# Neighbour-maximum stage: the row gathers of a tile are paced by all eight transpose steps

## The chip, the cores and the metric

The kernel runs on one core of one Trainium2 chip. The metric is device time in microseconds (us), median of several executions. Engines are named as in the profile: PE (TensorE), DVE (VectorE), ACT (ScalarE), POOL (GpSimd), SP (SyncE, here only DMA issues).

## What is computed

Four graph layers run over 8192 nodes with 128 features and one 8192 x 8192 adjacency matrix `adj` of int32 (about 33 neighbours in a row: each off-diagonal entry is set with probability 0.0039). Layer 0 is the one that the change touches; layers 1 to 3 are attention layers over the same mask.

```python
# layer 0: maximum over the neighbours, feature by feature
vals = jnp.max(jnp.where(mrows[:, :, None], X[None, :, :], neg), axis=1)
out  = jnp.where(has_nbr[:, None], vals, 0)
x = _layernorm(x + out)
# layer 1: attention with a threshold; layers 2 and 3: plain masked attention
attention = softmax(where(adj > 0, leaky_relu(s_i + s_j), NEG)) ; h = attention @ (x @ W)
x = _layernorm(x + elu(h))
```

## The kernel before

**The stage.** `neighbour_max` works in 64 row tiles of 128 nodes. PE transposes a tile of `adj` (1 MB a piece, four pieces) in eight steps `e` = 0 to 7 of eight 128x128 blocks (`turn`, L474), ACT turns each step's block into an fp8 mask (`stage`, L430), and every fourth tile the mask of four tiles goes to DRAM for the later layers. Neighbours are handled in groups of 16 columns ("words"). The first neighbour of each word is selected with matrix products: PE marks it (`first_ps`, L493), ACT makes it a 0/1 matrix (`lone`, L417), PE multiplies x with it (`sums`, L507), and DVE folds the result into a running maximum `top` (`pair`, L607, eight per tile, one per step). These are for the quad of four tiles before. Words with more than one neighbour leave neighbours over; DVE extracts up to 24 of them per node as row numbers (`idx`, L686 to L774), and POOL fetches these rows of x by indirect DMA into `ring` (24 slots of 128x128 fp32, one gather a slot, L356). DVE reduces `ring` by a tree of maxima (`larger`, L612, seven per tile) and writes the result (`into`, L619, two per tile).

**The order around the gathers.** PE, ACT and DVE go through phases, one per tile, each written out by hand as eight steps. DVE's phase t does three things interleaved: eight `pair` operations, the extraction of tile t-1, and the tree of tile t-3. POOL runs a loop over tiles, `tile(t, k)`. For tile t it waits until the indices exist (`idx_ready`) and then fills three ranges of the ring, each after the tree of tile t-1 has let it go:

- slots 6 to 11 ("upper"), free after the first L612 of a DVE phase (`upper_free`);
- slots 0 to 5 ("lower"), free after the first L619 (`lower_free`), after step 1;
- slots 12 to 14 ("rest"), free after the second L619 (`rest_free`), between steps 4 and 5;
- slots 15 to 23, three conditional groups of 2, 2 and 5 slots: gathered if any node of the tile needs them, else filled with -3e38 by a memset (L392).

`follow(part)` holds POOL until PE has finished `t * 8 + 16 + part` transpose steps: `part` = 0 is satisfied when PE's phase t+1 is over, `part` = p when step p-1 of phase t+2 is. The last two tiles are not paced.

**What waits for the gathers.** DVE's tree of tile t runs in phase t+3. Its first L612 waits for the twelve upper and lower gathers (`gathered`). Its fourth L612 (written at L726, after step 3) waits for `rest_ready`, which POOL gives in `report()`: that call waits until the rest and conditional gathers of the tile before have landed, and stands inside the next tile's program, between its upper and its lower gathers. Nothing but DVE waits for a gather; POOL's waits are for DVE and PE.

Of the kernel before, what the change touches and what calls it, by code (L numbers as in the profile page):

```python
# [33 lines left out]
HALF = SLOTS // 2  # L34
# [44 lines left out]
def hold(eng, sem, value):  # L79


    eng.wait_ge(sem, value)
    if not isinstance(value, int):
        eng.sem_inc(SPARE[0], 1)
# [96 lines left out]
def neighbour_max(nc, x, adj, mask_t, x_ext, nm, deg, consts, constants):  # L181
# [14 lines left out]
    with ExitStack() as ctx:  # L196
# [76 lines left out]
        gathered = sem("gathered")  # L273
# [21 lines left out]
        @block.sync  # L295
        def _(sp):
            for h in range(PIECES):
                sp.dma_start(adjb[:, h, :], adj[0:P, h * PW:(h + 1) * PW]).then_inc(adj_in[h], 16)

            def rows(t):  # L300

                for h in range(PIECES):

                    hold(sp, transposed, (t - 1) * 8 + (h + 1) * HT)
                    sp.dma_start(adjb[:, h, :], adj[bass.ds(t * P, P), h * PW:(h + 1) * PW]).then_inc(adj_in[h], 16)

            for t in range(1, TC):
                for k in SPLIT_BEHIND[t]:
                    quarter = slice(k * T // XQ, (k + 1) * T // XQ)
                    sp.dma_start(nm[:, quarter, :], x.rearrange("(t p) f -> p t f", p=P)[:, quarter, :]).then_inc(x_in[k], 16)  # L310
                rows(t)
            with sp.Fori(TC, T) as t:
                rows(t)

            sp.wait_ge(transposed, T * 8)
            sp.dma_start(x_again, x.rearrange("(t p) f -> p t f", p=P)).then_inc(x_back, 16)
            sp.wait_ge(flag_ready, 1)
            more = sp.value_load(flag[0:1, 0:1], min_val=0, max_val=1)
            with sp.If(more != 0):
                with sp.Fori(0, T) as t:  # L320
                    hold(sp, fb_adj_used, t + 1)
                    sp.dma_start(fb_rows, adj[bass.ds(t * P, P), :]).then_inc(fb_adj, 16)
                    with sp.Fori(0, N // FJ) as s:
                        hold(sp, fb_step, (t * (N // FJ) + s) * 3 + 1)
                        sp.dma_start(
                            xb, x[bass.ds(s * FJ, FJ), :].rearrange("j f -> (j f)").partition_broadcast(P),
                        ).then_inc(fb_x, 16)

        @block.gpsimd
        def _(pool):  # L330

            constants_on_pool(pool)
            pool.wait_ge(adj_in[PIECES - 1], 16)
            blocks = lambda ap: ap.rearrange("(a two p) f -> a two p f", two=2, p=P)
            for odd in range(2):
                pool.dma_start(blocks(x_ext[0:N, :])[:, 1 - odd], blocks(x)[:, odd]).then_inc(x_copied, 16)
            pool.wait_ge(low_ready, 1)
            pool.dma_start(x_ext[N:N + P, :], top[:, 0, 0:F]).then_inc(low_in, 16)
            sel_steps = Steps(pool, sel_made)
            sel_steps.do(nc.gpsimd.memset(sel[:, :, :], 0.0))  # L340
            for k in range(3):
                rows = range(3 * k, (3, 6, 7)[k])
                for at in range(0, P, 32):
                    for r in rows:
                        sel_steps.do(nc.gpsimd.affine_select(out=sel[:, k, :], in_=sel[:, k, :], compare_op=ALU.not_equal, fill=1.0, base=-(at + r), pattern=[[0, 1]], channel_multiplier=1))
            pool.wait_ge(x_copied, 32)
            pool.wait_ge(low_in, 16)
            blanks = Tally(pool, blanked, 1)
            extra = Tally(pool, low_in, 16)
            pool.sem_inc(blanked, 1)  # L350
            for free in (upper_free, lower_free, rest_free):
                pool.sem_inc(free, 1)

            def gather(k, first, number, done):
                for s in range(first, first + number):
                    pool.indirect_dma_start(ring[:, s, :], None, x_ext,  # L356
                                            bass.IndirectOffsetOnAxis(ap=idx[:, k, s:s + 1], axis=0)).then_inc(done, 16)

            def report():

                extra.wait(0)
                blanks.wait(0)
                pool.sem_inc(rest_ready, 1)

            def tile(t, k, paced=True):

                def follow(part):
                    if paced:
                        hold(pool, transposed, t * 8 + LATER * 8 + part)

                hold(pool, idx_ready, t + 1)
                hold(pool, upper_free, t + 1)
                for part in range(2):
                    follow(part)
                    gather(k, HALF // 2 + 3 * part, 3, gathered)
                report()
                hold(pool, lower_free, t + 1)
                for part in range(3):
                    follow(2 + part)
                    gather(k, 2 * part, 2, gathered)  # L380
                hold(pool, rest_free, t + 1)
                gather(k, FIRST[1], SIZES[1], low_in)
                pool.reg_add(extra.reg, extra.reg, 16 * SIZES[1])
                hold(pool, need_in, t + 1)
                for g in range(SURE, GROUPS):
                    rows = pool.value_load(need_i[0:1, k, g - SURE:g - SURE + 1], min_val=0, max_val=P)
                    with pool.If(rows != 0):
                        gather(k, FIRST[g], SIZES[g], low_in)
                        pool.reg_add(extra.reg, extra.reg, 16 * SIZES[g])
                    with pool.If(rows == 0):  # L390

                        nc.gpsimd.memset(ring[:, FIRST[g]:FIRST[g] + SIZES[g], :], -BIG).then_inc(blanked, 1)  # L392
                        pool.reg_add(blanks.reg, blanks.reg, 1)

            with pool.Fori(0, T // 2 - 1) as it:
                tile(it * 2, 0)
                tile(it * 2 + 1, 1)
            tile(T - 2, 0, False)
            tile(T - 1, 1, False)
            report()  # L400
            pool.wait_ge(x_back, 16)
            for quad in range(NC - 1):
                at = slice(quad * TC, (quad + 1) * TC)
                pool.wait_ge(rows_step, quad + 1)
                nc.gpsimd.tensor_tensor(out=nm[:, at, :], in0=nm[:, at, :], in1=x_again[:, at, :], op=ALU.add).then_inc(x_added, 1)
            pool.wait_ge(missed_ready, 1)
            nc.gpsimd.partition_all_reduce(missed_all[:, :], missed[:, :], P, bass.bass_isa.ReduceOp.max).then_inc(missed_shared, 1)
# [1584 lines left out]
```

## Time and profile before

| | |
|---|---|
| median of 3 executions | 4901.41 us (4897.9 to 4901.55) |
| span of the profiled execution | 5439.8 us |
| layer 0 in it | about 0 to 2240 us |
| layers 1 to 3 in it | about 2240 to 5440 us |
| busy in the span | PE 84%, DVE 79%, ACT 41%, POOL 22% |
| POOL | 1051 gathers, 148 memsets in the ring |

The profiled execution is 538.4 us longer than the median of the timed ones, so intervals in it can't be carried over to the timed ones without a look at where that time lies. Idle time of an engine that is not the bottleneck costs nothing; "issue" means that the engine waited for nothing the profile shows, and "remote" means that what released it wasn't found among the records near by.

### The profile page before, as it was taken

The numbers are of one execution on the slowest core, as the hardware profiler recorded it, in microseconds if no ns is written. First come the engines' busy times: TensorE is split into PE (matmuls) and PEld (weight loads), VectorE is DVE, ScalarE is ACT, GpSimd is POOL, SyncE is SP. The second block draws the span as 40 slices with busy tenths as digits, with TensorE's granted clock in tenths as the row PEclk, the third lists the DMA queues.
The fourth block names the chain that finished last, engine by engine and source line by source line (L and its number), as shares of the span: only waits on it lengthen the run. The fifth ranks groups of instructions, "written<-read, shape, count | busy, mean of one in ns | idle before, by whom it ended". The sixth has DMA issues, their size and how long they took to land. (4 is left out here: it accounts for less than half of the span.)

```text
span 5439.8 us, 68010 instructions
## 1 busy us (share of the span) xinstructions
PE 4559.6 (84%) x22263; PEld 2172.7 (40%) x22263; DVE 4311.2 (79%) x7371; ACT 2207.6 (41%) x2430; POOL 1205.9 (22%) x1342
## 2 busy tenths in 40 slices
PE   4766776677667766579999999999999999999999
PEld 3333333333333333323443333454444445444444
DVE  6666676667666667788888888889999987999998
ACT  3444444444444444398888888410000001000000
POOL 5555445454444455200000000000000000000000
PEclk6888888888888889889999999999999999999999
DMA  7555555555555555233232332122222202212220
GB/s 272 195 187 184 192 197 185 187 182 194 186 179 188 193 169 166 95 130 122 105 126 111 113 127 105 64 102 83 75 84 79 81 9 99 102 70 98 76 96 14
DMA packets 181695, 709.72 MB, mean 130 GB/s; under 512 B 31168, under 2 KB 39872, under 8 KB 132224
## 3 DMA queue, kind: packets, MB, share of 16 engines
q1 hardware_dynamic: 110816, 566.01, 29.3%
q0 software_dynamic: 33760, 73.21, 4.2%
q10 hardware_dynamic: 36864, 67.13, 3.5%
q8 instruction: 157, 2.57, 0.2%
q14 instruction: 98, 0.80, 0.0%
HBM read 630.59 MB, written 79.82 MB: 131 GB/s over the span
## 5 line engine op out<-in xcount | busy, mean ns | idle before, releaser
L1750 PE MATMUL bank<-w,GX 128*128 128x512 f32 x4096 | 1768.4, 593 | 4.8 <-DVE w L1865 4.8
L1865 DVE SCALAR_TENSOR_TENSOR w<-q,E,m 128x512 f32<-128x512 f32 x2048 | 1472.1, 758 | 130.8 <-PE bank L1750 39.1
L356 POOL DMA_INDIRECT ring<-x_ext,idx x1051 | 1032.8, 983 | 1074.2 <-DVE X L619 316.8
L1750 PEld LDWEIGHTS bank<-w,GX 128*128 128x128 f32 x4096 | 777.7, 191 | 975.3 <-issue 975.2
L607 DVE TENSOR_TENSOR top<-top,sums 128x1024 f32<-128x1024 f32 x484 | 589.2, 1217 | 626.7 <-remote 364.8
L507 PE MATMUL sums<-lone,xs 128*128 128x512 fp8e4 x3000 | 838.3, 421 | 287.0 <-DVE top L607 214.9
L1200 PE MATMUL acc<-w,GX 128*128 128x512 f32 x2048 | 939.6, 605 | 65.8 <-DVE w L1458 62.6
L430 ACT ACTIVATE stage<-tp 128x1024 fp8e4<-128x1024 uint16 x512 | 523.7, 1025 | 1088.1 <-remote 598.3
L1458 DVE SCALAR_TENSOR_TENSOR w<-q,E,u 128x1024 f32<-128x1024 f32 x512 | 634.7, 1274 | 1.9 <-PE acc L1200 1.8
L507 PEld LDWEIGHTS sums<-lone,xs 128*128 128x128 bf16 x3000 | 291.5, 105 | 814.7 <-issue 607.4
L1200 PEld LDWEIGHTS acc<-w,GX 128*128 128x128 f32 x2048 | 371.9, 190 | 564.5 <-issue 413.5
L417 ACT ACTIVATE lone<-first_ps 128x1024 fp8e4<-128x1024 f32 x512 | 522.3, 1020 | 83.1 <-PE first_ps L493 39.3
L1231 ACT ACTIVATE above<-q,nd 128x1024 fp8e4<-128x1024 f32 x488 | 516.7, 1142 | 0.0
L1242 ACT ACTIVATE u<-ell,ndd 128x1024 fp8e4<-128x1024 f32 x448 | 478.1, 1141 | 43.7 <-DVE w L1458 43.4
L493 PE MATMUL first_ps<-stage,firsts 128*128 128x512 fp8e4 x1022 | 343.7, 421 | 144.4 <-ACT lone L417 125.2
L474 PE MATMUL tp<-ident_b,adjb 128*128 128x128 bf16 x4096 | 361.8, 237 | 121.0 <-issue 54.6
L1762 ACT ACTIVATE num<-bank 128x512 f32<-128x512 f32 x32 | 19.1, 597 | 1006.4 <-PE bank L1750 1006.4
L1715 POOL TENSOR_TENSOR lone_part<-mean_w,nohas 128x512 f32<-128x512 f32 x32 | 37.7, 1180 | 1583.8 <-DVEq L1823 1561.1
L474 PEld LDWEIGHTS tp<-ident_b,adjb 128*128 128x128 bf16 x4096 | 276.5, 106 | 163.2 <-issue 71.2
L486 PE MATMUL tally<-powers,stage 128*128 128x16 bf16 x4096 | 169.9, 171 | 143.1 <-ACT stage L430 99.4
L486 PEld LDWEIGHTS tally<-powers,stage 128*128 128x128 fp8e4 x4096 | 163.9, 99 | 255.4 <-ACT stage L430 124.5
L612 DVE TENSOR_TENSOR ring<-ring 128x128 f32<-128x128 f32 (+2 forms) x448 | 251.2, 561 | 6.2 <-DMA ring<-x_ext,idx 3.6
(250 smaller groups left out, 2919.3 us busy)
## 6 DMA issues: line engine op xcount, KB each, us to landing
adjb<-in_adj SPq DMA_DIRECT2D x256, 1024.0 KB
m<-mask_t SPq DMA_DIRECT2D x128, 1024.0 KB, 4.8
mask_t<-stage ACTq DMA_DIRECT2D x256, 256.0 KB
den_m<-mask_t SPq DMA_DIRECT2D x64, 1024.0 KB, 6.9
keep_m<-mask_t SPq DMA_DIRECT2D x64, 1024.0 KB, 4.9
ring<-x_ext,idx POOLq DMA_INDIRECT x1051
z<-row_scores SPq DMA_DIRECT2D x30, 256.0 KB, 4.6
xt_rows<-XT SPq DMA_DIRECT2D x8, 512.0 KB, 4.7
```

What stands on the lines that cost most here:

```text
L356: pool.indirect_dma_start(ring[:, s, :], None, x_ext, bass.IndirectOffsetOnAxis(ap=idx[:, k, s:s + 1], axis=0)).then_inc(done, 16)
L417: nc.scalar.activation(lone[:, b, :, :], first_ps[:, :, :], ACT.Relu, saturate=False).then_inc(lone_made, 1)
L430: nc.scalar.activation(stage[:, q, e * TRB:(e + 1) * TRB, k * P:(k + 1) * P], tp[e % 2][:, :, :].bitcast(U16), ACT.Sign, saturate=False).t ...
L474: last = nc.tensor.transpose(tp[e % 2][:, i, :], low_half[:, j // PW, j % PW:j % PW + P], ident_b[:, :])
L507: last = nc.tensor.matmul(out[:, a, :], xs[:, part_, 2 * n + a, :], lone[:, b, a, :], start=(part_ == 0), stop=(part_ == 2))
L607: nc.vector.tensor_tensor(out=top[:, :, :], in0=top[:, :, :], in1=sums, op=ALU.max).then_inc(sums_used, 1)
L1200: last = nc.tensor.matmul(acc[:, h, :], GX[:, j, :], w[:, n % WR1, h, :], start=(j == 0), stop=(j == T - 1))
L1231: nc.scalar.activation(above[:, n % AS, :, i, :], qb[:, c % 2, :, :], ACT.Sign, bias=nd[:, j:j + 1], scale=-1.0, saturate=False).then_inc( ...
L1242: nc.scalar.activation(u[:, n % US, :, i, :], ell[:, c % 2, :, :], ACT.Sign, bias=ndd[:, j:j + 1], saturate=False).then_inc(keeps_made, 1)
L1458: nc.vector.scalar_tensor_tensor(out=w[:, n % WR1, :, :], in0=qb[:, c % 2, :, :], scalar=E[:, j:j + 1], in1=u[:, n // GT % US, :, j % GT, ...
L1750: last = nc.tensor.matmul(acc[b][:, :], GX[:, j, :], w[:, j % WR, :], start=(j == 0), stop=(j == T - 1))
L1865: nc.vector.scalar_tensor_tensor(out=w[:, j % WR, :], in0=q, scalar=E[:, j:j + 1], in1=m[:, b, j, :], op0=ALU.max, op1=ALU.mult).then_inc( ...
```

## The change

Only `tile` in POOL's program changes. The upper slots go in three pairs behind steps 0, 1 and 2 of PE's phase (before: two lots of three, behind the end of the phase before and behind step 0), and `report()` is called after the second pair, that is after four upper gathers and not after six. The lower slots go in pairs behind steps 3, 4 and 5 (before: 1, 2 and 3). The rest group gets a wait for step 6 on top of `rest_free`, and the conditional groups a wait for step 7, the last of the phase.

```diff
                 hold(pool, upper_free, t + 1)
-                for part in range(2):
-                    follow(part)
-                    gather(k, HALF // 2 + 3 * part, 3, gathered)
-                report()
+                for part in range(3):
+                    follow(1 + part)
+                    gather(k, HALF // 2 + 2 * part, 2, gathered)
+                    if part == 1:
+                        report()
                 hold(pool, lower_free, t + 1)
                 for part in range(3):
-                    follow(2 + part)
+                    follow(4 + part)
                     gather(k, 2 * part, 2, gathered)
                 hold(pool, rest_free, t + 1)
+                follow(7)
                 gather(k, FIRST[1], SIZES[1], low_in)
                 pool.reg_add(extra.reg, extra.reg, 16 * SIZES[1])
                 hold(pool, need_in, t + 1)
+                follow(8)
                 for g in range(SURE, GROUPS):
```

In the built program this is POOL's order from the top of a tile in the loop, before. `transposed` is PE's count of steps, `low_in` and `blanked` are what `report()` waits for.

```order
L82 ISA [waits idx_ready,upper_free]
L356 DMA ring<-x_ext,idx 128x128 [waits transposed]
L356 DMA ring<-x_ext,idx 128x128 x2
L82 REGISTER_ALU
L356 DMA ring<-x_ext,idx 128x128 [waits transposed]
L356 DMA ring<-x_ext,idx 128x128 x2
L82 REGISTER_ALU [waits low_in,blanked,lower_free]
L356 DMA ring<-x_ext,idx 128x128 [waits transposed]
L356 DMA ring<-x_ext,idx 128x128
L82 REGISTER_ALU
```

And the same place now:

```order
L82 ISA [waits idx_ready,upper_free]
L356 DMA ring<-x_ext,idx 128x128 [waits transposed]
L356 DMA ring<-x_ext,idx 128x128
L82 REGISTER_ALU
L356 DMA ring<-x_ext,idx 128x128 [waits transposed]
L356 DMA ring<-x_ext,idx 128x128
L82 REGISTER_ALU [waits low_in,blanked]
L356 DMA ring<-x_ext,idx 128x128 [waits transposed]
L356 DMA ring<-x_ext,idx 128x128
L82 REGISTER_ALU [waits lower_free]
```

The report has moved ahead of the last two upper gathers, and these have a wait of their own. Further down in POOL's tile, at the rest group and the first conditional one, this stood before:

```order
L356 DMA ring<-x_ext,idx 128x128 [waits rest_free]
L356 DMA ring<-x_ext,idx 128x128 x2
L383 REGISTER_ALU
L386 TENSOR_LOAD need_i [waits need_in]
L386 ISA x2
```

And now:

```order
L82 REGISTER_ALU [waits rest_free]
L356 DMA ring<-x_ext,idx 128x128 [waits transposed]
L356 DMA ring<-x_ext,idx 128x128 x2
L385 REGISTER_ALU
L82 REGISTER_ALU [waits need_in]
L389 TENSOR_LOAD need_i [waits transposed]
L389 ISA x2
```

Both groups now wait for a step of PE after the wait that they had. No instruction of PE, DVE, ACT or SP moves.

## Rows read from the trace of the kernel before

**Rows 1.** The page: length of the profiled execution.

```profile
span 5439.8 us, 68010 instructions
```

**Rows 2.** Busy time of each engine in a stretch of layer 0, granted clock, DMA share.

```profile
500.00:1000.00 500.00, 350.14 (x2852) 180.41 (x2851) 340.37 (x711) 234.51 (x265) 249.70 (x279) 0.87 0.55 188
```

**Rows 3.** Groups by line, 0 to 2400 us: count, busy, mean; idle before, releasers.

```profile
L356 POOL DMA_INDIRECT ring<-x_ext,idx x1051 | 1032.8, 983 | 1074.2 <-DVE X L619 316.8 <-issue 306.5 <-DVE ring L612 193.2
...
L607 DVE TENSOR_TENSOR top<-top,sums 128x1024 f32<-128x1024 f32 x484 | 589.2, 1217 | 626.7 <-remote 364.8 <-PE sums L507 227.2 <-issue 33.0
```

**Rows 4.** Waits of DVE, 200 to 2100 us: total, times, longest.

```profile
DVE top L607 <- remote: 335.8, 90, 10.1
DVE top L607 <- PE sums L507: 206.2, 205, 3.1
```

**Rows 5.** Line 356, the gathers: durations min/median/max, and who waited for them.

```profile
L356 POOL DMA_INDIRECT ring<-x_ext,idx x1051: 938/944/3283, 41.0 to 2193.7; - x176
...
who waited for it (us, times):
  DVE ring L612: 3.6, 1
```

**Rows 6.** Tile X and line 711: durations min/median/max, first and last start.

```profile
L619 DVE TENSOR_TENSOR X<-ring x64: 278/280/851, 78.8 to 2205.7; 128x128 f32<-128x128 f32 x64
...
L711 DVE TENSOR_SCALAR keys<-codes x64: 413/426/552, 22.2 to 2148.3; 128x512 int32<-128x512 int32 x64
```

**Rows 7.** Timeline around 1010 us: start, us, engine, line.

```profile
1001.20 0.95 DVE L612 TENSOR_TENSOR ring<-ring 128x768 f32<-128x768 f32 x1
...
1005.71 0.61 PE L474 MATMUL tp<-ident_b,adjb 128*128 128x128 bf16 x8
...
1006.23 0.94 POOL L356 DMA_INDIRECT ring<-x_ext,idx  x1 [7.13 <-DVE X L619]
...
1009.13 0.61 PE L474 MATMUL tp<-ident_b,adjb 128*128 128x128 bf16 x8
...
1013.69 0.95 DVE L612 TENSOR_TENSOR ring<-ring 128x768 f32<-128x768 f32 x1
...
1014.64 0.61 PE L474 MATMUL tp<-ident_b,adjb 128*128 128x128 bf16 x8
...
1021.33 0.61 PE L474 MATMUL tp<-ident_b,adjb 128*128 128x128 bf16 x8
1021.37 1.21 DVE L607 TENSOR_TENSOR top<-top,sums 128x1024 f32<-128x1024 f32 x1
```

**Rows 8.** The same timeline a few steps on.

```profile
1029.96 1.02 ACT L430 ACTIVATE stage<-tp 128x1024 fp8e4<-128x1024 uint16 x1 [9.28 <-remote]
...
1030.08 1.22 DVE L607 TENSOR_TENSOR top<-top,sums 128x1024 f32<-128x1024 f32 x1 [5.70 <-remote]
...
1030.72 0.94 POOL L356 DMA_INDIRECT ring<-x_ext,idx  x1 [2.37 <-remote]
```

**Rows 9.** Timeline of DVE, first phase after the last transposes.

```profile
2141.81 0.95 DVE L612 TENSOR_TENSOR ring<-ring 128x768 f32<-128x768 f32 x1
...
2149.39 1.21 DVE L607 TENSOR_TENSOR top<-top,sums 128x1024 f32<-128x1024 f32 x1
...
2153.56 0.95 DVE L612 TENSOR_TENSOR ring<-ring 128x768 f32<-128x768 f32 x1
```

**Rows 10.** Timeline of POOL, the same phase, and after the last gather.

```profile
2143.52 0.95 POOL L356 DMA_INDIRECT ring<-x_ext,idx  x1 [5.17 <-DVE ring L612]
...
2147.27 0.96 POOL L356 DMA_INDIRECT ring<-x_ext,idx  x1 [0.30 <-issue]
...
2149.87 0.94 POOL L356 DMA_INDIRECT ring<-x_ext,idx  x1 [0.30 <-issue]
...
2158.13 0.94 POOL L356 DMA_INDIRECT ring<-x_ext,idx  x1 [0.30 <-issue]
...
2196.67 16.90 POOL L405 TENSOR_TENSOR X<-X,adjb 128x512 f32<-128x512 f32 x12 [0.86 <-DMA ring<-x_ext,idx]
```

## The prediction

> **What bounds the kernel now.** I read the span first, then the busy times of a stretch of layer 0, then the groups by line, then who waits for whom, and last the timeline of single phases. Only layer 0 holds gathers; the three layers behind it are not touched by an instruction and are taken as they are.
>
> The profiled execution takes 5439.8 us [rows 1], 538.4 us more than the median of 4901.41 us. In layer 0 the first L619 of a tile starts 64 times between 78.8 and 2205.7 us [rows 6], so a phase takes (2205.7 - 78.8) / 63 = 33.8 us in the trace. A phase without disturbance can be pieced together from the rows. From the start S of a phase (the first L612, three quarters of 1024 wide) to the fourth L612 (L726, after step 3) DVE needs 2153.56 - 2141.81 = 11.75 us [rows 9]; that phase has no transposes, but its first part takes as long as one that has them: 7.58 us to the `pair` of step 2 there, 1021.37 - 1013.69 = 7.68 us here [rows 7, 9]. From L726 to the next phase's start DVE needs 1013.69 - 1001.20 = 12.49 us [rows 7]. Together 24.2 us. The missing 9.6 us of a phase are in holes: at 1021.94 us PE ends a transpose step, and ACT, DVE and POOL start again only at 1029.96, 1030.08 and 1030.72, all three put down to "remote" [rows 7, 8]. DVE's waits of that kind sum to 335.8 us [rows 4]. Such holes over 63 phases are 63 x 9.6 = 605 us, near the 538.4 us by which the profiled execution is longer. So I take nearly all of the holes to be absent from the timed executions. A timed phase is then about 33.8 - 538.4 / 63 = 25.2 us.
>
> What fills it is DVE: it is busy 340.37 of 500 us in the trace [rows 2], 68% of 33.8 us, that is 23.0 us of work per phase, 91% of 25.2 us. The rest is mostly DVE waiting for PE's sums (206.2 us over some 56 phases, holes included, all of it before L607) [rows 3, 4]. POOL is busy 250 of 500 us, 16.9 us a phase [rows 2], its idle time before gathers is put down to DVE's L619 and L612 first [rows 3], and DVE waited for a gather once, 3.6 us [rows 5]. So layer 0 goes at DVE's pace with PE close behind, and POOL has about 8 us a phase to spare. A change of POOL's order counts only if it makes DVE wait, or ends a wait of DVE.
>
> **The change part by part.** All times are from S; a timed phase ends at S + 25.2 and its undisturbed bound is S + 24.2.
>
> *Upper gathers.* POOL's first one starts at 2143.52, S + 1.71 (0.76 us after that L612 ended), and then one every 1.25 us [rows 9, 10]. PE's step 1 ends at 1014.64 + 0.61 = S + 1.56, step 3 at 1021.33 + 0.61 = S + 8.25 [rows 7]; step 0 is over before S, and step 2 lies between, near S + 5. The new gates ask for step 0 before the pair at S + 1.7, step 1 before that at S + 4.2 and step 2 before that at S + 6.7. All are open when POOL comes to them. Cost 0.
>
> *The report.* It came after the sixth gather, whose start is 2149.87 and end 2150.81, S + 9.0; DVE asks at S + 11.75, so the margin is 2.75 us and DVE did not wait. Now it comes after the fourth, 2147.27 + 0.96, S + 6.4, margin 5.3 us [rows 9, 10]. Gain 0 where there was no wait. The one tile whose big conditional group was gathered (148 memsets of 192 leave 44 gathered groups, and 1051 - 960 = 91 gathers in them make 43 groups of two and one of five) may have had one: at most the 3.6 us of [rows 5], once.
>
> *Lower gathers.* Before, the sixth started at 2158.13, S + 16.3, and ended at S + 17.3 [rows 10]. The gates now are step 3 (S + 8.25), step 4 (a step is 24.2 / 8 = 3.0 us, S + 11.3) and step 5 (S + 14.3), against pairs that started at S + 9.3 (2149.87 + 1.25), S + 11.8 (two gathers on) and S + 15.1 (2158.13 - 1.25). An open gate costs nothing; a gate that POOL waits at lets it go about 1 us later (0.76 us from the end of the L612 to the first upper gather above). So the last pair may slip from S + 15.1 to S + 15.3, and end at S + 17.6. What is the landing? After POOL's last gather (start 2193.7 [rows 5], end 2194.6) it waited until 2196.67 for the data, memsets in between, so landing is at most 2.1 us [rows 10]. The twelve are there at S + 19.7, and DVE asks for them at S + 24.2 at the earliest: margin 4.5 us. Cost 0. The Trainium skill says in "Perfetto Trace Analysis" (the part on the DMA instruction of the software path) that the profiler's end of such an instruction is the end of descriptor generation and not the arrival of the data; the row on 2196.67 agrees, which is why the 2.1 us stand in the margin.
>
> *Rest group.* `rest_free` let POOL start at 1006.23, 5.03 us after L726, hence S + 16.8, or at S + 17.6 when the lower gathers end later. Step 6 ends at 1005.71 + 0.61, 5.12 us after L726, S + 16.9 [rows 7]. If POOL has to wait there, it starts 1 us later, S + 17.9: a slip of 0.3 to 1.1 us, with 3 x 1.25 us of gathers behind it, end S + 21.6. Nobody waits for them before S + 24.2 + 11.75. Cost 0.
>
> *Conditional groups.* Step 7 ends at 1009.13 + 0.61 = 8.54 us after L726, S + 20.3 [rows 7], before POOL gets there. With memsets (about 1.2 us) POOL is done at S + 22.8, with one gathered pair (2.5 us more) at S + 25, with two at S + 27. The next upper gathers can't start before S + 24.2 + 1.7 = S + 25.9. Queued behind this wait on POOL are those next upper gathers and the report; the worst common case pushes them by 1 us against a margin of 5.3 us. Cost 0 in 63 tiles, and 0 to 5 us once in the tile with nine extra gathers.
>
> *Added waits themselves.* Three more register waits a tile on POOL, some tenths of a us each, in 8 us of spare time: 0.
>
> The bounds: a row that shows a paced gather making DVE wait does not exist, so its cost is bounded above by the 1 us that a closed gate takes, if all of it reached DVE in every phase, 62 us; the bound below is the part of a timed phase over the undisturbed one, 25.2 - 24.2 = 1.0 us a phase, 63 us, if smoother gathers removed all of it. I take 0, since every margin is over 4 us. Sum: 5439.8 + 0 for a profiled execution, 4901 us timed (before's own spread is 3.7 us; what can be told from no change is about 0.2%, 10 us).
>
> One rule speaks for more than that. A gather takes 0.94 us as a rule and up to 3.28 us [rows 5], so something blocks POOL at times; the one DVE operation of 0.43 us per phase of the tensor-scalar kind, L711, takes 0.41 to 0.55 us [rows 6]. The Trainium skill, "SBUF — State Buffer", Who interferes with whom, says that a VectorE operation in a two-port mode and GpSimd exclude each other from a shared port pair, the loser standing still. By that rule a moved gather can lose or gain one L711, 0.4 us of POOL's spare time, and DVE at most 0.14 us a phase (0.55 - 0.41), 9 us in all; the upper gathers lie under L711 before and after, so neither changes here.
>
> **The rivals.** *R1, faster: bursts of gathers are what holds the others up.* The holes lie at steps 3 and 4, after POOL has issued eight or more gathers in a row, and the steps in which POOL is idle are quick. If part of this is real in timed executions, pairs spread over the phase would give it back. The pot is the 1.0 us a phase: all of it 63 us, 4838 us; a third to a half, 4870 to 4880 us. Against it: the gates are open when POOL comes, so the burst of twelve is hardly broken up; it decides only if PE's steps come later than POOL's pace, above all where a hole has already begun. *R2, slower: the gates bind and DVE waits.* Place: the last lower pair behind step 5 and the first L612 of the next phase. If PE in timed executions runs late against DVE (its clock is granted at 0.87 on the mean here [rows 2]) by more than 4.5 us at step 5, each phase pays the excess; 0.5 us a phase gives 31 us, 4932 us. Against it: DVE waits for each step's sums, so PE can't be a whole step and a half behind. *R3, slower: the conditional groups next to the phase change.* 44 groups; if each moved the report past its margin by 0.5 us it would be 22 us, 4923 us. It decides once POOL is more than 5.3 us late, which only the nine-gather tile is. *R4: the change does in effect nothing*, gates open throughout: that is the forecast, with no difference in time.
>
> **How the numbers follow.** Forecast and R4 together 0.53, at 4901 us, own range 4893 to 4910. R1 0.29, R2 0.12, R3 0.06. The range takes most of R1 and the near half of R2 and R3: 4868 to 4922. Faster by over 0.2%: 0.29; within 0.2%: 0.53; slower: 0.18.
>
> **What would show it.** In the changed profile: the sixth upper gather of a tile still 6.4 us after the first; the first L612 and L726 of a phase with no wait for a gather or POOL; POOL's waits before L356 moving from L619 and L612 towards PE's L474; 1051 gathers and 148 memsets; undisturbed pieces of 11.75 and 12.5 us as before. The place and size of the holes may differ, and with them the profiled span, without a change in the timed median. The forecast is wrong if the undisturbed pieces change, if DVE waits for a gather in many phases, or if the timed median moves with the holes; the last would say that the holes are in the timed executions too.

## The result, and the profile after

The changed kernel takes 4924.65 us (median of 4; 4922.01 to 4927.49) against 4901.48 us before: ratio 1.0044, 95% interval 1.0029 to 1.0059. Measured once more beside the last experiments it is 4924.21 us, ratio 1.0049 (1.0036 to 1.0063). It is slower by 20 to 24 us, outside the range forecast. Ratios and intervals here and below are of undisturbed executions: one of the kernel before (5138 us) and two of the variant b_stt (7550 and 13435 us) were slow and are left out of them, and the median of b_stt without those two is 4896.66 us.

Its profiled execution takes 4921.2 us and has no holes, so the trace that stands ahead of the prediction can't be compared with it row by row. The kernel before was profiled again, unchanged ("b_again" below), this time without holes: 4900.3 us. "Before" in the rows from here on is this second trace. The two pages, first the changed kernel, then before:

```profile
span 4921.2 us, 68382 instructions
```

```profile
span 4900.3 us, 68010 instructions
```

DVE's waits from 200 to 1600 us, changed kernel and then before (us in total, times, longest). In place of the 335.8 us "remote" and 206.2 us for PE's sums of [rows 4] there is this:

```profile
DVE top L610 <- PE sums L510: 90.6, 165, 3.6
DVE ring L615 <- DMA ring<-x_ext,idx: 1.5, 2, 1.2
```

```profile
DVE top L607 <- PE sums L507: 84.9, 168, 3.2
DVE ring L612 <- DMA ring<-x_ext,idx: 3.1, 1, 3.1
```

DVE waits 5.7 us more for PE's sums, which comes back at the end of this document, and less than before for gathers: no wait explains 23 us. What grew most is the duration of one tiny DVE operation, which writes the 128x3 flags `need` and stands between the last `pair` of a phase and `idx`. These are its rows by line (min/median/max in ns; L771 in the changed kernel, L768 before):

```profile
L771 DVE TENSOR_SCALAR need<-srt x64: 158/182/1628, 31.1 to 1660.0; 128x3 bf16<-128x3 f32 x64
```

```profile
L768 DVE TENSOR_SCALAR need<-srt x64: 156/164/1630, 31.0 to 1637.2; 128x3 bf16<-128x3 f32 x64
```

The medians hide it. Over 0.3 us it takes in 30 of 64 tiles after and in 20 before, and summed over its own median it has 23.3 us too much after, 9.4 us before. The timeline of one tile with one gathered pair shows where it comes from. Changed kernel, end of a tile (start, us, engine, line):

```profile
686.68 0.61 PE L477 MATMUL tp<-ident_b,adjb 128*128 128x128 bf16 x8
687.14 0.94 POOL L356 DMA_INDIRECT ring<-x_ext,idx  x1 [0.30 <-issue]
...
688.71 0.94 POOL L356 DMA_INDIRECT ring<-x_ext,idx  x1 [0.62 <-issue]
...
689.96 0.94 POOL L356 DMA_INDIRECT ring<-x_ext,idx  x1 [0.31 <-issue]
690.68 0.18 DVE L769 SCALAR_TENSOR_TENSOR base<-srt,four 128x24 int32<-128x24 int32 x1
690.86 0.97 DVE L771 TENSOR_SCALAR need<-srt 128x3 bf16<-128x3 f32 x1
690.90 0.90 POOL L395 MEMSET ring<- 128x256 f32 x2
...
691.99 0.95 DVE L615 TENSOR_TENSOR ring<-ring 128x768 f32<-128x768 f32 x1
```

The same place before, in another tile with one gathered pair:

```profile
172.44 0.61 PE L474 MATMUL tp<-ident_b,adjb 128*128 128x128 bf16 x8
172.83 0.94 POOL L356 DMA_INDIRECT ring<-x_ext,idx  x1 [0.30 <-issue]
174.07 0.94 POOL L356 DMA_INDIRECT ring<-x_ext,idx  x1 [0.30 <-issue]
175.32 0.94 POOL L356 DMA_INDIRECT ring<-x_ext,idx  x1 [0.30 <-issue]
176.26 0.90 POOL L392 MEMSET ring<- 128x256 f32 x2
...
176.63 0.56 DVE L768 TENSOR_SCALAR need<-srt 128x3 bf16<-128x3 f32 x1
...
177.35 0.95 DVE L612 TENSOR_TENSOR ring<-ring 128x768 f32<-128x768 f32 x1
```

The line of a memset x2 stands for two of them, 128x256 (group of two) and 128x640 (group of five). In both kernels the small operation ends within 0.05 us of the end of the second one (691.80 and 177.16): DVE stands until POOL has finished. Before, the memset is 0.37 us ahead of the operation and costs it 0.4 us; after, it starts 0.04 us behind, directly after a gather, and costs 0.8 us. Everything behind it on DVE, the next phase included, starts later by as much. In the tiles without a gathered pair the memsets are over before L771 in both kernels (0.17 us).

That it is the memset and not the gather ahead of it can be seen in three tiles of the changed kernel in which more than one conditional group is gathered. There a gather ends 0.04 us behind the start of the operation, just as above, but another gather follows it and no memset, and the operation takes 0.17 us; with memsets behind the gather it takes 0.95 to 0.97 us, in 25 tiles. One of the three:

```profile
333.14 0.94 POOL L356 DMA_INDIRECT ring<-x_ext,idx  x1 [0.30 <-issue]
334.04 0.17 DVE L771 TENSOR_SCALAR need<-srt 128x3 bf16<-128x3 f32 x1
334.39 0.94 POOL L356 DMA_INDIRECT ring<-x_ext,idx  x1 [0.30 <-issue]
```

Why the memset is later is seen at POOL's sequencer. It loads the flag of each conditional group, branches, and goes on to the next. These are its three loads in the two tiles above, changed kernel and then before (the times are the first and last start):

```profile
L389 POOLq TENSOR_LOAD <-need_i x3: 283/291/293, 687.4 to 690.1; - x3
```

```profile
L386 POOLq TENSOR_LOAD <-need_i x3: 284/287/296, 170.4 to 173.0; - x3
```

Before, the sequencer runs ahead of the engine: the loads start at 170.4, under the first rest gather and 3.7 us before the first conditional one (174.07), and the last of them is done before that one starts. After, the sequencer stands at the new wait for step 7, whose last transposes end at 687.29, and only then begins: first load at 687.4, last at 690.1. The first conditional gather starts 0.62 us after the rest group (0.30 before).

This moves the end of the memsets by 0.4 us in the tiles in which they lay on the operation before too. In seven tiles (counted from 0: 15, 19, 31, 35, 43, 51 and 60) they were over 0.24 us ahead of the operation before, and now they lie on it for 0.97 us. In six of the seven the operation stands at the end of the first phase of a quad, and in such a phase the new gates do hold POOL. These are the third upper pair and the first lower pair in the phase that ends with the operation of tile 15, changed kernel:

```profile
418.30 0.94 POOL L356 DMA_INDIRECT ring<-x_ext,idx  x1 [1.24 <-PE tp L477]
...
421.56 1.26 POOL L356 DMA_INDIRECT ring<-x_ext,idx  x1 [1.07 <-PE tp L477]
```

A second difference is at the start of the kernel. DVE's waits from 60 to 110 us, the changed kernel and then before:

```profile
DVE ring L615 <- DMA ring<-x_ext,idx: 7.3, 2, 5.5
```

```profile
DVE ring L612 <- DMA ring<-x_ext,idx: 3.6, 1, 3.6
```

The first gather starts at 50.7 us and not at 41.0 us, since the first tile's upper pair now needs step 0 of phase 2, and PE's early phases wait for the adjacency tiles to come in. DVE's first `pair` starts at 103.9 us against 101.1 us.

### The profile page after: what moved, and what is told of

It reads as the page before. It is cut to its first block and busy times, and to the rows that moved or that the text cites. A ratio compares the mean times of both kernels' runs of the same rounds, so it can differ in the third digit from the quotient of the medians.

```text
span 4921.2 us, 68382 instructions
## 1 busy us (share of the span) xinstructions
PE 4381.2 (89%) x22263; PEld 2106.9 (43%) x22263; DVE 4321.6 (88%) x7371; ACT 2210.7 (45%) x2430; POOL 1232.6 (25%) x1342
## 5 line engine op out<-in xcount | busy, mean ns | idle before, releaser
L356 POOL DMA_INDIRECT ring<-x_ext,idx x1051 | 1060.2, 1009 | 507.7 <-issue 295.4
L510 PE MATMUL sums<-lone,xs 128*128 128x512 fp8e4 x3000 | 742.1, 384 | 261.7 <-DVE top L610 237.7
L510 PEld LDWEIGHTS sums<-lone,xs 128*128 128x128 bf16 x3000 | 262.6, 98 | 740.0 <-issue 441.3
L477 PE MATMUL tp<-ident_b,adjb 128*128 128x128 bf16 x4096 | 327.0, 225 | 71.0 <-DVE X L633 38.0
L496 PE MATMUL first_ps<-stage,firsts 128*128 128x512 fp8e4 x1022 | 311.0, 386 | 0.3 <-ACT lone L420 0.3
L477 PEld LDWEIGHTS tp<-ident_b,adjb 128*128 128x128 bf16 x4096 | 254.1, 101 | 102.5 <-DVE X L633 41.3
L615 DVE TENSOR_TENSOR ring<-ring 128x128 f32<-128x128 f32 (+2 forms) x448 | 250.5, 559 | 15.4 <-DMA ring<-x_ext,idx 12.8
L1769 ACT ACTIVATE ex<-ex 128x512 f32<-128x512 f32 x32 | 20.2, 630 | 540.0 <-DVE ex L1827 540.0
```

The lines of the kernel that those rows point to most:

```text
L356: pool.indirect_dma_start(ring[:, s, :], None, x_ext, bass.IndirectOffsetOnAxis(ap=idx[:, k, s:s + 1], axis=0)).then_inc(done, 16)
L477: last = nc.tensor.transpose(tp[e % 2][:, i, :], low_half[:, j // PW, j % PW:j % PW + P], ident_b[:, :])
L510: last = nc.tensor.matmul(out[:, a, :], xs[:, part_, 2 * n + a, :], lone[:, b, a, :], start=(part_ == 0), stop=(part_ == 2))
```

## The experiments

Changes are against the kernel named. Excess means the time by which the small operation (L768 or its line in the variant) takes longer than its own median in that trace, summed over the tiles in which it does.

**b_again, the kernel before, unchanged, one execution.**

> The kernel before, unchanged, profiled once more to get a phase without the holes that its first trace had. Theory A (collision: POOL's memset of a conditional group holds up DVE's small tensor-scalar L768, as it does in 30 tiles of the changed kernel, 0.98 us in place of 0.17): span near 4900 us, L768 long in fewer than 10 tiles or by clearly less, phases shorter than after's by 0.37 us on the mean. Theory B (the later gathers land later and DVE waits for data): L768 as long as after's, and L612 waits for the gathers' DMA less than the 12.8 us in the changed kernel.

Measured: 4902.06 us, span 4900.3 us. From DVE's first `pair` to the next phase's, a phase takes 25.2 us on the mean (25.5 us in the changed kernel). The operation is long in 20 tiles, not fewer than 10, but at 0.56 us in most and not 0.97 us. The wait of DVE for gathers is less than after (10.7 against 12.8 us in all), a difference of 2 us that lies at the start. Theory A is favoured, with a part of the cost already in the kernel before.

**no8, the changed kernel without the wait for step 7.**

```diff
                 hold(pool, need_in, t + 1)
-                follow(8)
                 for g in range(SURE, GROUPS):
```

> The changed kernel without the wait for step 7 ahead of the conditional groups. The wait adds 0.30 us between the rest gathers and the conditional ones (0.61 us against 0.31 us) although its step is long over. Theory A: the memsets come 0.3 us earlier against L771, which then takes 0.67 us in place of 0.97 us in about 28 tiles: 8 us less, 4916 us. Theory B (late data): under 2 us less.

Measured: 4915.17 us, ratio to before 1.0026 (1.0017 to 1.0035). The operation takes 0.64 to 0.67 us in 24 tiles; excess 14.2 us, 9 us less than after; the time is 9 us less. As A said.

**no78, without the waits for steps 6 and 7.**

```diff
                 hold(pool, rest_free, t + 1)
-                follow(7)
                 gather(k, FIRST[1], SIZES[1], low_in)
                 pool.reg_add(extra.reg, extra.reg, 16 * SIZES[1])
                 hold(pool, need_in, t + 1)
-                follow(8)
                 for g in range(SURE, GROUPS):
```

> The changed kernel without the waits for steps 6 and 7: what is left of the change is the pairs behind later steps and the early report. Theory A: the memsets come 0.4 us earlier, L771 loses some 0.35 us in 28 tiles, not 0.8 us: 4912 to 4914 us, unless the chain ahead of it moves too. Theory B: 4922 us or so if the later lower pairs are what costs, 4901 us if the rest group is.

Measured: 4908.03 us, ratio 1.0013 (1.0004 to 1.0022), better than the 4912 to 4914 us expected: the operation is at 0.56 us again, but in 28 tiles and not 20 (excess 12.4 us, 3 us over before). The seven tiles named above are among them, so the later gates of the pairs are enough to bring the memsets onto the operation there (0.56 to 0.57 us). The upper and lower gates and the early report together are worth 7 us at most: nearly 3 us are the start and 3 us this. Against no8 the time is 7 us less, while the excess is only 2 us less; the profiled executions of the two take equally long in layer 0 (1594 and 1595 us from the first `pair` to the last), so what else the wait for step 6 costs, if anything, isn't shown.

**a_stt, the changed kernel with the small operation in another form.** It compares twice, (srt < 1) < srt, which gives the same 0 or 1.

```diff
-nc.vector.tensor_scalar(need[...], srt[...], 1.0, None, ALU.is_ge)
+nc.vector.scalar_tensor_tensor(out=need[...], in0=srt[...], scalar=1.0, in1=srt[...],
+                               op0=ALU.is_lt, op1=ALU.is_lt)
```

> The changed kernel with the small DVE operation at L771 in another form that gives the same numbers (a scalar-tensor-tensor, which compares twice), everything else as it is. Theory A: if only the tensor-scalar form has to share with POOL's memset, the new one takes 0.17 us in all tiles, and the 23 us go: 4901 us or a little less. Theory B: no difference, 4924 us.

Measured: 4897.18 us, ratio 0.9991 (0.9982 to 1.0): all of the loss is gone. The same place in a tile, its timeline:

```profile
178.57 0.95 POOL L356 DMA_INDIRECT ring<-x_ext,idx  x1 [0.30 <-issue]
...
179.48 0.15 DVE L771 SCALAR_TENSOR_TENSOR need<-srt 128x3 bf16<-128x3 f32 x1
179.52 0.90 POOL L395 MEMSET ring<- 128x256 f32 x2
179.55 0.17 DVE L773 SCALAR_TENSOR_TENSOR base<-srt,base 128x24 int32<-128x24 int32 x1
```

```profile
L771 DVE SCALAR_TENSOR_TENSOR need<-srt x64: 151/157/193, 30.6 to 1631.0; 128x3 bf16<-128x3 f32 x64
```

The memset starts 0.04 us behind the operation, exactly as in the changed kernel, and the operation takes 0.15 us: at most 0.193 us in 64 tiles. All of POOL's work is where the change put it. This is the run that settles the cause.

**b_stt, the same edit in the kernel before.**

> The kernel before with the small DVE operation at L768 in its scalar-tensor-tensor form. In before's trace without holes L768 is long too: 0.56 us in 20 tiles, 9.4 us over its usual 0.16 us. Theory A (collision with the memset): these 9 us go, 4892 us. Theory B (the changed kernel lost 23 us through late data, and the other form only happened to win it back): no change, 4901 us.

Measured: 4897.75 us, ratio 0.9987 (0.9974 to 1.0). The direction is A's; the size, some 5 to 6 us, is less than the 9 us expected. With this form in both, the changed kernel (4897.18) and the one before (4897.75) can't be told apart.

**b_rev, the kernel before with the conditional groups in reversed order.**

```diff
-                for g in range(SURE, GROUPS):
+                for g in reversed(range(SURE, GROUPS)):
```

> The kernel before with the three conditional groups in reversed order: the group of five first, then the two of two. In tiles with one gathered pair (always the first of the two) the memsets then come before the pair and are over some 2 us ahead of L768, which keeps its form. Theory A: L768 takes 0.16 us in nearly all tiles, 4892 us. Theory C (it is the gathers and not the memsets that hold the operation up): the pair now lies over L768, which gets longer, 4901 us or more.

Measured: 4896.8 us, ratio 0.9985 (0.9976 to 0.9995). The expectation was right in time and half right in the trace: L768 is still long in 22 tiles, in 21 of them at about 0.4 us (excess 5.6 us), although no memset is near:

```profile
174.31 0.90 POOL L392 MEMSET ring<- 128x640 f32 x2
...
176.63 0.94 POOL L356 DMA_INDIRECT ring<-x_ext,idx  x1 [0.30 <-issue]
...
177.16 0.41 DVE L768 TENSOR_SCALAR need<-srt 128x3 bf16<-128x3 f32 x1
```

It ends with the gather (177.57): a gather holds it up too, theory C, but less than the memsets do, and only with its last part. In this trace the operation ends with the gather in 22 of the 23 tiles in which it starts 0.53 to 0.72 us into one, and takes its usual 0.16 to 0.17 us where it starts 0.05 to 0.33 us into one. The gain comes from moving the memsets off it.

**b_gate1, the kernel before with later gates for the upper gathers alone.**

```diff
                 for part in range(2):
-                    follow(part)
+                    follow(1 + part)
```

> The kernel before, its two upper lots of three behind steps 0 and 1 of PE's phase and not behind the end of the phase before and step 0. In the changed kernel the first tile's gathers start at 50.7 us and not at 41.0 us, and DVE waits 5.5 us for them and not 3.6 us. Start-up theory: the first pair of DVE comes some 2.5 us later here as there, L768 is as in before: 4904 us. If it is 4901 us, the start-up costs nothing; if it is 4910 us or more, the gates of the upper gathers cost in the other tiles too.

Measured: 4905.64 us, ratio 1.0009 (0.9996 to 1.0023): the time fits but alone can't be told from no change. The trace is clearer: first gather at 50.8 us, first `pair` at 104.2 us (101.1 before), excess of L768 8.2 us, no more than before. DVE's wait from 60 to 110 us:

```profile
DVE ring L612 <- DMA ring<-x_ext,idx: 7.0, 2, 4.3
```

**b_plus8, the kernel before with the wait for step 7 alone.**

```diff
                 hold(pool, need_in, t + 1)
+                follow(8)
                 for g in range(SURE, GROUPS):
```

> The kernel before with the wait for step 7 alone, ahead of the conditional groups. It should shift the memsets by 0.3 us towards the end of the tile. Theory A: L768 goes from 0.56 us to 0.87 us in the 20 tiles in which it was long, 6 us more: 4907 us. Theory B (late lower gathers): no change, 4901 us.

Measured: 4919.07 us, ratio 1.0027 (1.0018 to 1.0037). The wait does more than expected: the operation goes to 0.97 us in 25 tiles, excess 22.5 us, 13.1 us over before. One line makes most of the loss. It too brings the memsets onto the operation in the seven tiles in which they were ahead of it, at 0.96 us: either this wait or the later gates of the pairs is enough for that. Later gates for the upper gathers alone (b_gate1) leave it at 0.16 us in all seven.

```profile
174.85 0.95 POOL L356 DMA_INDIRECT ring<-x_ext,idx  x1 [0.69 <-issue]
176.10 0.94 POOL L356 DMA_INDIRECT ring<-x_ext,idx  x1 [0.30 <-issue]
...
177.00 0.97 DVE L769 TENSOR_SCALAR need<-srt 128x3 bf16<-128x3 f32 x1
177.04 0.90 POOL L393 MEMSET ring<- 128x256 f32 x2
```

The gap ahead of the conditional gather is 0.69 us and not the 0.61 us I had expected from a fixed cost: POOL is released by an event, the end of step 7, and lands in the same place whether the rest gathers end 0.1 us earlier or not. So the step was not "long over", as the expectation for no8 has it.

**a_loads, the changed kernel with the three flag loads ahead of the wait.**

```diff
+                wanted = [pool.value_load(need_i[0:1, k, g - SURE:g - SURE + 1], min_val=0, max_val=P) for g in range(SURE, GROUPS)]
                 follow(8)
                 for g in range(SURE, GROUPS):
-                    rows = pool.value_load(need_i[0:1, k, g - SURE:g - SURE + 1], min_val=0, max_val=P)
+                    rows = wanted[g - SURE]
```

> The changed kernel with the three loads of the conditional groups' flags ahead of the wait for step 7; the wait itself stays. Run-ahead theory: POOL's sequencer reaches this wait under the running rest gathers, at S + 18.5, and stands there until step 7 (S + 20.4); only then come three times load, check and branch, 0.9 us each, so that the last memset can't start before S + 24.0. With the loads done ahead it can: first conditional gather at S + 21.45, memset over 0.3 us earlier, L771 0.65 us, 4915 us as without the wait. Rival (the gate itself and its register arithmetic make the delay): no change, 4924 us.

Measured: 4914.05 us, ratio 1.0025 (1.0015 to 1.0035), what no8 has without the wait. The wait is there, behind the same step, and costs nothing of its own once the loads are ahead of it:

```profile
178.90 0.94 POOL L356 DMA_INDIRECT ring<-x_ext,idx  x1 [0.30 <-issue]
179.84 0.90 POOL L396 MEMSET ring<- 128x256 f32 x2
...
180.11 0.65 DVE L772 TENSOR_SCALAR need<-srt 128x3 bf16<-128x3 f32 x1
```

**a_again and a_stt_g0.** The changed kernel unchanged, beside these, and the changed kernel with the other form and with its upper gates one step earlier (`follow(part)` in place of `follow(1 + part)`).

> The changed kernel, unchanged, beside the next ones on the same chip: 4922 to 4927 us as before, L771 long (0.97 us) in about 30 tiles.

> The changed kernel with the other form of L771 and with its upper pairs behind parts 0, 1 and 2 and not 1, 2 and 3: no collision, and the first tile's gathers start at 41 us again. Start-up theory: 2.5 to 3 us less than with the other form alone (4897 us): 4894 us. If it stays at 4897 us the start-up term is made good later.

Measured: 4924.21 us, excess 23.1 us over 30 tiles, and 4895.93 us, ratio of the latter 0.9983 (0.9975 to 0.9992). That is the direction of the start-up theory, but 1.3 us between two medians, of runs on different chips, is within their scatter, so in time the start-up term stays between nothing and 3 us; in the traces it is seen each time.

| kernel | us | ratio to before | excess of the small operation |
|---|---|---|---|
| before | 4901.5 | 1 | 9.4 |
| changed | 4924.65 | 1.0044 | 23.3 |
| b_plus8 | 4919.07 | 1.0027 | 22.5 |
| no8 | 4915.17 | 1.0026 | 14.2 |
| a_loads | 4914.05 | 1.0025 | 14.1 |
| no78 | 4908.03 | 1.0013 | 12.4 |
| b_rev | 4896.8 | 0.9985 | 5.6 |
| b_stt | 4897.75 | 0.9987 | 0 |
| a_stt | 4897.18 | 0.9991 | 0 |
| a_stt_g0 | 4895.93 | 0.9983 | 0 |

The variants ran on three chips, on which the kernel before itself had medians of 4901.14 us (b_again, no8, no78, a_stt), 4902.56 us (the other variants of before) and 4904.33 us (a_again, a_loads, a_stt_g0), so the ratios compare better than the times. They aren't the quotients of these medians: for b_plus8 that would be 1.0034. The excess is over a median that is itself between 0.16 and 0.21 us; over 0.16 us throughout, the sums are 9.6 us before, 24.2 us for the changed kernel, 22.8 us for b_plus8, 15.9 us for no8, 16.0 us for a_loads and 13.0 us for no78, in the same order.

The last four beat the kernel before by a small amount; for the two stt forms the interval reaches 1. The differences among the four are not measured.

## Why the prediction was wrong

*What held.* A timed phase was put at 25.2 us, with an undisturbed bound of 24.2 us; the trace without holes has 25.2 us, and 24.3 us in its quick tiles. The holes were absent from the timed executions. POOL's pace, the times of L726, of the steps and of `rest_free` came out within 0.3 us of those written down. The report and the landing of data cost nothing in the steady state. Of the slower rivals, R2 is refuted in its consequence, since DVE does not wait for a gather (1.5 us in 200 to 1600 us), though its premise, gates that bind, holds in the first phase of a quad. R3 had the right place, the conditional groups beside the phase change, and even the time, 4923 us, but by a mechanism that the traces don't show: no report came too late for DVE in the usual tile, so that the time fits is luck. R1, faster by smoother gathers, had nothing to win: a_stt and b_stt are the same.

*The step that failed* is the one on the conditional groups: "Step 7 ends at ... S + 20.3, before POOL gets there. With memsets ... POOL is done at S + 22.8, with one gathered pair ... at S + 25 ... Cost 0". The term was put at nothing; b_plus8, with this wait alone, measures it at 13 to 17 us, of which 13.1 us are seen as excess. Two things are wrong in it.

First, "before POOL gets there" holds for the engine and not for its sequencer. The sequencer stood at this point from about S + 18.5 on, by the start of POOL's last register instruction ahead of the wait. I read a gate as open when the engine's next instruction came after it. But what follows the gate is work of the sequencer, three loads with check and branch at 0.9 us each, which used to run ahead under the gathers. The wait took that cover away, and the memsets start 3.6 us after step 7 (690.90 - 687.29). I had called the added waits free because of "8 us of spare time". b_plus8 shows what the wait does, a_loads that it is the lost run-ahead.

Second, I asked mainly who waits for POOL's work. A POOL operation holding up DVE I bounded only with L711, the wide one, which hardly changes (at most 0.55 us in [rows 6]), and the small L768 I did not look at. Its row in the first trace would hardly have warned me:

```profile
L768 DVE TENSOR_SCALAR need<-srt x64: 160/163/854, 31.1 to 2173.4; 128x3 bf16<-128x3 f32 x64
```

It is long there in one tile of 64, since the holes make a phase 33.8 us and POOL is done well before the operation; the second trace of the same kernel has 20. My own numbers had POOL done at S + 25 in the tiles with a pair, which is what the trace has (24.9), and DVE's phase ending at S + 24.2: they overlap just where L768 stands, 0.4 us ahead of the next phase where nothing holds it up. The Trainium skill, "SBUF — State Buffer", Who interferes with whom, says that of a VectorE operation in a two-port mode and a GpSimd operation the one that issues first has the shared pair and the other one stands for the whole instruction, and it counts the tensor-scalar kind among those that can need the pair. The traces agree that DVE's operation stands until POOL has finished: 0.97 us in place of 0.16 us under two memsets of 0.90 us. That the one issued first wins they don't show: by the rows the operation starts 0.04 us ahead of the memset, and it is the operation that stands. For an operation with two inputs from SBUF the page has contention only with a GpSimd operation that reads SBUF, which a memset does not; the scalar-tensor-tensor form took 0.15 us in the same place. The page's rule was in the prediction, weighed for the wrong operation.

A smaller step failed in the same way: "All are open when POOL comes to them" for the upper gathers, and gates that bind at the last lower pair alone, were worked out for one phase. In the first phase of a quad the gates do hold POOL (1.24 and 1.07 us in the rows above). DVE still waits for no gather, but the memsets come later and onto the operation, 3 us of excess in no78.

*The first tile.* "Cost 0" for the upper gathers was worked out for a steady phase. In the first tile the gate holds POOL nearly 10 us longer than before, and DVE's first `pair` is 2.8 us later. I had the row, a first gather at 41.0 us [rows 5], and did not ask what released it.

*The sum.* At the last `pair` the traces of before and after differ by 22 us. Of these 2.8 us are the start and 13.9 us the excess (23.3 - 9.4). The rest is about 5 us. It builds up in one place: the first phase of every quad, between `pair` 0 and `pair` 1, 5.59 us on the mean of 14 against 5.03 us, 8 us in all, of which some 2 to 3 us are made good in the last eight phases. Where this gap is long, PE's granted clock is low; a short one and a long one of before, and a long one of after (the clock is the third number from the end):

```profile
910.00:914.30 4.30, 2.30 (x19) 1.35 (x19) 2.84 (x7) 1.64 (x2) 3.05 (x4) 1.00 0.32 57
707.70:713.60 5.90, 4.07 (x20) 1.94 (x21) 2.66 (x7) 1.94 (x2) 2.50 (x3) 0.71 0.35 86
```

```profile
923.80:929.40 5.60, 3.73 (x20) 2.05 (x21) 2.70 (x6) 1.94 (x2) 3.50 (x4) 0.70 0.37 83
```

PE stands ahead of these places for DVE, 38.0 us in 14 waits after and 37.5 us before, so equally long, and then works at a granted clock of 0.70 to 0.71 on the mean in the long gaps shown, so partly at 1.2 GHz and not 2.4 GHz, and of 1.00 in the short one. The gap is long in 12 of 14 quads after and in 8 of 14 before. The other traces speak for a link with the long `need` operation. Summed over the 14 quads the gap takes 77 to 80 us in the three traces in which the operation is at 0.97 us (the changed kernel twice, b_plus8), and 66 to 74 us in the nine others. a_stt, with the same order on POOL as the changed kernel, is at 69 us. How a stop of 0.8 us on DVE would lower PE's clock is not shown, and so some 5 us of the loss are explained only in place. In no8 a part is open as well: 4.8 us more excess than before and 2.8 us for the start, 13 us measured.

## What to carry to other kernels

A wait in front of work of the sequencer (a load into a register, a branch) costs more than its own time: it ends the run-ahead, so put the loads ahead of it. When an engine's instructions are moved in time, ask of each what lies beside it on the other engine at the new place and which of the two can stop, in both directions; a median hides an operation that is six times as long in nearly half of its instances, so look at the largest duration and at a timeline, in a trace whose span agrees with the timed median. And an operation of 0.16 us on the engine that sets the pace is worth a form that POOL doesn't stop.

## What the runs showed of the hardware

- POOL's memsets (0.90 us for one of 128x256 and one of 128x640) stop a DVE tensor-scalar operation of 128x3 elements until they end: 0.97 us and not 0.16 us. The scalar-tensor-tensor form in the same place was not held up (0.15 to 0.19 us in all 64 tiles of a_stt). The last part of a gather holds the tensor-scalar form up as well, by some 0.25 us in b_rev; operations that started at most 0.33 us into a gather were not held up there.
- POOL's sequencer runs far ahead of its engine: 3.7 us in the tile shown, with three loads of 0.29 us and their branches done under gathers.
- One profiled execution of a kernel can be 538 us longer than its timed ones, with holes in which three engines restart together, and the next one of the same kernel not at all (5439.8 and 4900.3 us).
